# Causal attention in a post-norm layer: one mask product per maxima bank, and the first diagonal key tile laid out by query halves

## What is computed

```python
q = (x @ wq).reshape(b, s, NH, HD)
k = (x @ wk).reshape(b, s, NKV, HD)
v = (x @ wv).reshape(b, s, NKV, HD)
scores = jnp.einsum('bihd,bjhd->bhij', q, k) * SCALE
causal = jnp.tril(jnp.ones((s, s), dtype=bool))
scores = jnp.where(causal, scores, jnp.finfo(scores.dtype).min)
attn = jax.nn.softmax(scores, axis=-1)
out = jnp.einsum('bhij,bjhd->bihd', attn, v)
```

## Time and profile before

| | |
|---|---|
| median of 3 runs | 3632.71 us |
| the profiled execution, its own time | 3631.32 us |
| its span, first to last instruction | 3629.2 us |
| mean granted TensorE clock | 0.986 |
| TensorE products, busy | 3517.4 us (97%), 26506 of them |
| TensorE weight loads | 2460.0 us (68%) |
| VectorE, ScalarE, GpSimd busy | 1927.5, 1491.4, 1559.7 us |
| maxima scores L532 | 2560, mean 421 ns |
| maxima masks L535 | 1024, mean 236 ns |
| attention, from first to last product | 550 us to 2693 us |

### The profile page before, as it was taken

One profiled execution on the slowest core, in us unless ns is written; L12 is line 12 of the kernel. 1 busy time (PEld: TensorE's weight loads), 2 busy tenths in 40 slices (PEclk: granted clock), 3 DMA queues, 4 the chain that ended last, 5 costly groups with the idle time before them and its releaser, 6 DMA issues. The chain is left out here.

```text
span 3629.2 us, 64158 instructions
## 1 busy us (share of the span) xinstructions
PE 3517.4 (97%) x26506; PEld 2460.0 (68%) x26506; DVE 1927.5 (53%) x3577; ACT 1491.4 (41%) x1839; POOL 1559.7 (43%) x672
## 2 busy tenths in 40 slices
PE   8999998999999999999999999999969999999999
PEld 7888885555565565665665556556537888888887
DVE  3121217666666666666666666666615666642223
ACT  3111112555555555555555555555542222221111
POOL 0000002767867777787786787787530000000000
PEclk9999997999999999999999999999989999999999
DMA  6343325021111111111112111110027777755553
GB/s 209 119 128 113 112 86 114 23 50 48 34 41 48 39 34 50 47 31 44 48 31 50 48 33 41 48 38 9 12 81 199 231 228 225 213 187 178 175 181 129
DMA packets 248227, 340.74 MB, mean 94 GB/s; under 512 B 55440, under 2 KB 150288, under 8 KB 247952
## 3 DMA queue, kind: packets, MB, share of 16 engines
q1 hardware_dynamic: 247952, 336.87, 31.6%
HBM read 203.08 MB, written 133.17 MB: 93 GB/s over the span
## 5 line engine op out<-in xcount | busy, mean ns | idle before, releaser
L674 DVE TENSOR_REDUCE p_part_max<-p_qm 128x1 f32<-128x512 f32 (+3 forms) x2240 | 1357.1, 669 | 716.5 <-PE p_qm L532 442.9
L503 POOL TENSOR_TENSOR p_psums<-p_psums,p_probs 128x1024 f32<-128x1024 f32 x560 | 1331.4, 2378 | 82.0 <-ACT p_probs L637 2.2
L637 ACT ACTIVATE p_probs<-p_km 128x1024 f32<-128x1024 f32 x1024 | 1032.0, 1024 | 542.5 <-PE p_km L556 438.1
L532 PE MATMUL p_qm<-p_k_st,p_q_st 96*128 96x512 f32 (+3 forms) x2560 | 916.4, 421 | 14.7 <-DMA p_q_st<-q_hi 10.7
L556 PE MATMUL p_km<-p_q_st,p_k_st 97*128 97x512 f32 x2048 | 714.5, 428 | 9.5 <-ACT p_probs L637 7.2
L532 PEld LDWEIGHTS p_qm<-p_k_st,p_q_st 96*128 96x128 f32 x2560 | 495.4, 196 | 230.8 <-DVE p_part_max L674 162.8
L566 PE MATMUL p_o<-p_probs,p_v 128*32 128x256 f32 (+1 forms) x9216 | 581.8, 371 | 0.0
L556 PEld LDWEIGHTS p_km<-p_q_st,p_k_st 97*128 97x128 f32 x2048 | 355.2, 192 | 156.3 <-issue 110.7
L499 POOL TENSOR_TENSOR p_psums<-p_probs 128x1024 f32<-128x1024 f32 x95 | 226.2, 2381 | 501.0 <-ACT p_probs L637 501.0
L566 PEld LDWEIGHTS p_o<-p_probs,p_v 128*32 128x32 f32 x9216 | 270.9, 110 | 213.6 <-issue 58.8
L41 PE MATMUL p_acc<-p_xT_hi,p_w_hi 128*128 128x512 f32 x640 | 250.1, 391 | 9.5 <-DVE p_w_lo L226 9.5
(11 more groups left out here) (152 smaller groups left out, 3958.3 us busy)
## 6 DMA issues: line engine op xcount, KB each, us to landing
p_q_st<-q_hi SPq DMA_DIRECT2D x128, 256.0 KB, 4.7
p_x_raw<-in_xT SPq DMA_DIRECT2D x64, 256.0 KB, 3.5
q_hi<-p_out_hi SPq DMA_DIRECT2D x64, 256.0 KB, 2.0
q_lo<-p_out_lo SPq DMA_DIRECT2D x64, 256.0 KB, 2.3
p_q_st<-q_lo SPq DMA_DIRECT2D x64, 256.0 KB, 4.4
attended_T<-p_o_raw SPq DMA_DIRECT2D x128, 128.0 KB
p_a_raw<-attended_T SPq DMA_DIRECT2D x32, 512.0 KB, 4.9
p_recip<-reciprocals SPq DMA_DIRECT2D x128, 128.0 KB, 6.7
```

What stands on the lines that cost most here:

```text
L503: pool.tensor_tensor(sums[:, :, :], sums[:, :, :], probs[s % PB][:, :, :], ALU.add).then_inc(added, 1)
L532: last = pe.matmul(bank[:, x * keys:(x + 1) * keys], q_st[par][0:ROWS, c, h + x, sub * P:(sub + 1) * P], k_st[par][0:ROWS, j * CK:j * CK + ...
L637: act.activation(probs[s % PB][:, :, :].rearrange("p h q -> p (h q)"), km[s % 2][:, :, :].rearrange("p a b -> p (a b)"), ACT.Exp, scale=SC ...
L674: dve.reduce_max(part_max[c][:, h:h + heads, sub, j], qm[bank_of(i)][:, 0:item_width(i)].rearrange("p (h k) -> p h k", h=heads), AX.X).the ...
```

## The change

In `item`, the score products of all heads of an item come first, only the first of them with the start flag, and one mask product for all heads follows. It repeats the 128-column mask for each head and writes to the last 128 keys of each, so it is 512 columns wide in one run (4 heads), 2 x 128 with a jump (2 heads), or 128 (1 head, as before). In `scores`, the first diagonal tile is laid out by query halves: bank 1 gets the later 128 queries of all 4 heads, bank 0 the earlier ones, and only bank 0 gets a mask, of 512 columns. The second diagonal tile moves to bank 1. The exp of the first diagonal tile reads both banks and writes each run of 128 to its place between the heads.

```diff
-                for x in range(item_heads(i)):
+                heads = item_heads(i)
+                for x in range(heads):
                     last = pe.matmul(bank[:, x * keys:(x + 1) * keys], q_st[par][0:ROWS, c, h + x, sub * P:(sub + 1) * P],
-                                     k_st[par][0:ROWS, j * CK:j * CK + keys], start=True, stop=j < c)
-                    if j == c:
-                        last = pe.matmul(bank[:, (x + 1) * keys - P:(x + 1) * keys], ident_bf[:, :], mask_q[:, :],
-                                         start=False, stop=True)
+                                     k_st[par][0:ROWS, j * CK:j * CK + keys], start=x == 0, stop=j < c)
+                if j == c:
+                    diagonal = bank[:, 0:heads * keys].rearrange("p (h k) -> p h k", h=heads)[:, :, keys - P:keys]
+                    last = pe.matmul(diagonal, ident_bf[:, :], mask_q[:, :].unsqueeze(1).to_broadcast([P, heads, P]),
+                                     start=False, stop=True)
...
-                if t == 2 * c + 1:
-                    four = pair[:, 0, :].rearrange("p (h q) -> p h q", h=REP)
-                    pe.matmul(four, keys, q_st[par][0:ROWS + 1, c // 2, :, q0 + P:q0 + CQ], start=True, stop=False)
+                if t >= 2 * c:
+                    first = t - 2 * c
+                    for x in range(1, first - 1, -1):
+                        four = pair[:, x, :].rearrange("p (h q) -> p h q", h=REP)
+                        last = pe.matmul(four, keys, q_st[par][0:ROWS + 1, c // 2, :, q0 + x * P:q0 + (x + 1) * P],
+                                         start=True, stop=x > first)
                     last = pe.matmul(four, ident_bf[:, :], mask_k[:, :].unsqueeze(1).to_broadcast([P, REP, P]),
                                      start=False, stop=True)
                 else:
...
-                                         start=True, stop=t < 2 * c)
-                        if t == 2 * c:
-                            last = pe.matmul(two[:, :, 0:P], ident_bf[:, :],
-                                             mask_k[:, :].unsqueeze(1).to_broadcast([P, 2, P]), start=False, stop=True)
+                                         start=True, stop=True)
...
-                if offset(s):
-                    act.activation(probs[s % PB][:, :, P:CQ], km[s % 2][:, 0, :].rearrange("p (h q) -> p h q", h=REP),
+                c, t = STEPS[s]
+                tile = probs[s % PB]
+                if t >= 2 * c:
+                    first = t - 2 * c
+                    act.activation(tile[:, :, first * P:CQ].rearrange("p h (x q) -> p x h q", q=P),
+                                   km[s % 2][:, first:2, :].rearrange("p x (h q) -> p x h q", h=REP),
                                    ACT.Exp, scale=SCALE).then_inc(exp_done, 1)
```

More of the change, by code:

```diff
@@ L632, in exps @@
                 act.wait_ge(scored, n * NS + s + 1)
-                if offset(s):
-                    act.activation(probs[s % PB][:, :, P:CQ], km[s % 2][:, 0, :].rearrange("p (h q) -> p h q", h=REP),
+                c, t = STEPS[s]
[4 more added lines that the diff above has]
+                                   km[s % 2][:, first:2, :].rearrange("p x (h q) -> p x h q", h=REP),
                                    ACT.Exp, scale=SCALE).then_inc(exp_done, 1)
                 else:
-                    act.activation(probs[s % PB][:, :, :].rearrange("p h q -> p (h q)"),
+                    act.activation(tile[:, :, :].rearrange("p h q -> p (h q)"),
                                    km[s % 2][:, :, :].rearrange("p a b -> p (a b)"),
```

## The result

The changed kernel takes 3620.4 us (median of 7 runs, 3619.0 to 3622.7) against 3632.7 us (7 runs): a ratio of 0.9965, 95% interval 0.9953 to 0.9976. The forecast was 3620.7. Several of its terms fit to some hundredths of a microsecond. But the sum lacked a loss, dips of the clock, and in the two profiles that loss was made up by clock time that the kernel before lost elsewhere.

A forecast was written before the change was run, and what follows sets the result against it. TensorE was taken to set the pace mostly, with GpSimd's chain and VectorE swallowing part. Groups 1 to 14 save 10.5 us, group 15 0.5, group 0 1.0: together 12.0, from 3632.7 to 3620.7 us; range 3608 to 3631.5.

The forecast's parts named there:

- The price of a product: Maxima products, TensorE time at their own place: 0.11 us saved with four heads, 0.12 with two.
- rival of slow weight loads: Scores side by side in the maxima products: loads take 0.19 us each, about 3632, no change; chance 0.12.
- The strided mask: Two-head mask writing two runs of 128 in a bank: taken to cost 0 extra.
- GpSimd's cover: Stretches 11 (third step) to 17 and next group's 0: savings only lengthen TensorE's wait, by some 0.5 us per group.
- VectorE's gates: VectorE's bank reads limit savings: 0.08 us counted in stretch 4, 0.22 in stretch 5.
- Sum per group: Stretches 4, 5, 9 and the key tiles: 0.08 + 0.22 + 0.35 + 0.10 = 0.75 us per group.
- the four key tiles: First diagonal key tile in stretches 1, 3, 7 and 10: 0.10 us saved per group.
- the clock: Rival: longer wait for GpSimd brings a dip of about 5 us in each group, 3691 us; chance 0.04.
- Group 0: First batch-head group, taken as mostly VectorE's: 1.0 us saved, between 0 and 3.

The follow-up runs named there:

- run 10: Changed kernel with 12 key tiles of chunk 7 summed by GpSimd and VectorE reading only half of each head's scores for the maxima: 3520.6 us.
- run 1: Kernel before, changed only outside GpSimd's chain: maxima items of chunks 0 and 3, first diagonal key tile of chunks 1 to 5: 3617.4 us.
- run 2: Kernel before, changed only under GpSimd's chain: maxima items of chunks 1 and 2, first diagonal key tile of chunks 0, 6 and 7: 3645.4 us.
- run 5: Kernel before, with 12 key tiles of chunk 7 summed by GpSimd in place of 13, the 13th by TensorE: 3621.6 us.
- run 6: Changed kernel, with 12 key tiles of chunk 7 summed by GpSimd in place of 13, the 13th by TensorE: 3596.2 us.
- run 4: Kernel before with only the first diagonal key tile changed, the maxima items as before: 3632.7 us, ratio 0.9996.

## Why the prediction was right

*The price of a product.* Right: with the gates off, in run 10, four heads save 0.11 (stretch 4, forecast 0.11) and two heads some 0.13 (stretches 5, 12 and 16, forecast 0.12), and scores side by side start 0.11 us apart, though each load's own row lasts 0.19. That rejects the rival of slow weight loads. The Trainium skill ("TensorE: Matmul & The Clock Gate", Part 3, the mechanism) has a load overlap running products "only when row_grp differs", and taken alone that doesn't hold for these loads. The same section also lets a load into the background weight buffer run ahead; the prediction left that out, and no row shows which buffer these loads used.

*The strided mask.* Right: no price. The 128 two-head masks in two runs are part of the savings above. The Trainium skill's sentence on non-contiguous PSUM access ("SBUF — State Buffer", the note on cachelines) doesn't hold for runs of 128 here: the mask in two runs lasts 0.28 us, as a plain 256-column product does.

*GpSimd's cover.* Right, and shown by runs 1, 2, 5 and 6: what stands under the chain only lengthens the wait, by 0.57 us where some 0.5 was forecast.

*VectorE's gates.* Right for the stretches 4 and 5 (0.07 and 0.26 against 0.08 and 0.22).

*Sum per group.* 0.75 forecast; 0.75 measured in the first profile (130.83 to 130.08, groups without a dip) and 0.71 in the second (130.12). Over 14 groups that is 10.0 to 10.4 us. Inside the sum the stretches 5 and 9 gave somewhat more than reckoned (0.26 for 0.22, 0.37 for 0.35) and the four key tiles less (0.04 for 0.10, though 0.11 in run 4).

*Wrong: the clock.* The rival priced one dip of 5 us in each group and had a chance of 0.04. What came lies between it and the forecast: 3 dips of 3.4 us, 1.4 us each, 4.2 us given back. The argument against it, that such waits already stood in every group at clock 1.00, took the old wait's length for the new one's. So the sum put at nothing what was 4.2 us.

*Group 0.* The term of 1.0 us (0 to 3) looks mis-sized, since the group became 4.5 us shorter, but an estimated 2.8 of that are the clock's, as shown above. Two other comparisons fit. With 12 tiles the group takes 185.4 us in the kernel before, 51.2 at half clock, and 182.5 in the changed one, 47.8 at half: 1.4 of the 2.9 are the clock's. And the key tile alone, which saves next to nothing, takes 189.3 with 61.4 at half, 2.7 more than the kernel before, where the clock would make it 2.8. What is left for the change is 1.5 to 1.7 us, an estimate within the range. I had put this group down as VectorE's, and no row was read for it.

*What was luck.* The dips took 4.2 us off the gain between the two profiles. The clock time that the kernel before lost in group 0 and in the feed-forward gave about as much back. The dips stand behind the wait that the change lengthened; nothing ties the other part to it. Whether the medians of seven runs hold the same two parts isn't shown. That the total hit to 0.3 us is worth less than it looks.

## What to carry to other kernels

Read a small product's price from start to start, its successor's included. Here a mask of 256 columns cost no more than one of 128, so batching short products saved the products and not their columns; that each costs the weight load behind it is the likely reason, not a shown one. Before adding up savings, look for another engine's unbroken chain over the same stretch: under it a saving was here not merely worth nothing, it lengthened a wait, and behind the longer wait the clock fell. Then move one piece of work off that chain: here a single tile was worth 10 us by itself, and the change on top of it 25 in place of 12.

## What was not expected

A wait of TensorE can cost more than its length. At the place of the wait for GpSimd the clock held at 1.07 to 1.19 us; at 1.55 to 1.65 it fell to half behind 2 or 3 of the 14 waits; at 4.5 with all, for 6.8 or 13.7 us. And VectorE's reads, whose waits of TensorE's products sum to only 0.5 us by the list of waits, held back 5.2 us per group. They show at the weight loads, not at the products; this row is from the kernel before with 12 tiles:

```profile
PEld p_qm L532 <- DVE p_part_max L674: 162.6, 474, 0.7
```

Such a row has to be read with the loads. Why group 0 carries its dip of 10 us in two profiles (the kernel before and the key tile alone), one of 3.4 in run 1 and none in the others stays open, and so does the length of the half clock at the attention's start.
